# Ordering the second graph's edges between the running sums of the first layer, with those sums written out

## The chip, the cores and the metric

The kernel runs on one core of one Trainium2 chip. The metric is device time in microseconds (us) from the first to the last instruction of one execution. The core has a matrix engine (PE, whose weight loads are listed as PEld), three engines for elementwise work (DVE, ACT, POOL) and SP, which here only issues DMAs. Each runs its own instruction stream. They are ordered by semaphores alone.

## The reference, cut to what matters

```python
def gcn_layer(x, src, dst, norm, W, b, n):        # three times; 12500 nodes, 200000 edges + self loops, 256 features
    h = x @ W
    msg = h[src] * norm[:, None]
    return segment_sum(msg, dst, n) + b           # gelu after the first two
x = x + gcn3(layernorm(x), src, dst)              # the first graph
# second graph: 131072 other edges (edge_index), only the router's attention uses them
alpha = softmax over the incoming edges of leaky_relu(a_src[src2] + a_dst[dst2])
scores = layernorm(segment_sum(h[src2] * alpha, dst2) + b_gat)
x = x + sum over the top 2 of 4 experts of gate * ffn_expert(layernorm(x))
```

Both edge lists must be ordered by their target before sums over the edges of a target can be made. The order of the second graph is first used after the third layer.

## The kernel before, in words

The program is a row of blocks. At the end of a block all engines meet.

1. Constants and weights.
2. `order_second` (called in L643, body from L310): the 131072 edges of the second graph as 128 rows of 1024 keys. DVE makes one-hot tiles (L210, L212, in a loop of 64) that PE multiplies to count the edges of each target (L224). Then comes a bitonic sort: `exchange` (L231, L232) is one min and one max over 128x512, with a wait on DVE's own semaphore behind it; fourteen times PE transposes the keys (L305, 8 transposes) and DVE reads them back from PSUM (L238 to L240). Its tiles lie in `acc`, a large SBUF tile.
3. `order_first`: the same preparation for the first graph, whose edges arrive sorted, so the sort is skipped. It starts with loads of the edges, and DVE waits for them (L509).
4. Normalisation of x and the table of features in HBM.
5. `layer(l)` (L741), three times. Partition p of the core walks over 1563 edges of its own. POOL issues one indirect DMA for each edge column (L824: 128 rows of 256 floats from `feature_table`), 16 of them to a chunk, into one of four row buffers (`rows_in`). DVE makes the running sum, one instruction for each edge column (L896): state = state * keep + row, into PSUM, 16 states. After each sum DVE waits on its own semaphore `s_c`. ACT copies four states at a time to one of four output buffers (L777), `sums_out`, two in `acc` and two in `work`, and stages the next indices for POOL (L769, `put`). SP writes each chunk, 2 MB, to HBM (L961). POOL may fill a row buffer again when DVE has counted it as used (`s_used`) and ACT has staged its indices. On DVE the chunks are a hardware loop (`dve.Fori(0, LAPS)`, 24 laps of 4 chunks, 64 sums in its body), followed by three smaller chunks written out (16, 8 and 3 sums). ACT, POOL and SP loop in the same way. After the sums the layer gathers one row per node (L853) and does its matmuls (L869, L879), the node part.
6. The attention table, then one large block: POOL's 1024 gathers for the second graph (L1205) beside the experts' matmuls on PE (L1284, L1294, a loop of two node pairs per lap), and at the end the router and the weighted sum of the experts on DVE (L1501 to L1576, written out, beside 98 gathers of L1220).

## Time and profile before

| | us |
|---|---|
| median of 3 runs (11795.35 to 11846.04) | 11817.82 |
| the profiled execution, its own time | 11829.28 |
| its span in the trace | 11827.6 |
| POOL busy | 5887.5 (50%) |
| DVE busy | 3860.8 (33%) |
| PE busy | 2554.4 (22%) |
| ACT busy | 1826.5 (15%) |

The span is the time from the first to the last instruction of one profiled execution. An engine's busy time leaves out register, branch and semaphore instructions and the issuing of DMAs by queues other than POOL's indirect ones. No engine is busy for more than half of the span, so the shares name no bottleneck, and each stage has to be read by itself. In the timelines a line is an instruction (or a run of equal ones), and the bracket at its end is the idle time of its engine ahead of it, with what ended it. "issue" is idle time that ended with nothing that the profile shows.

### The profile page before, as it was taken

To read this page: it belongs to the slowest core of one execution; us is meant where nothing else is said; L and a number is where in the kernel's file an instruction comes from. 1 tells how busy PE (TensorE), PEld (TensorE's weight loads), DVE (VectorE), ACT (ScalarE), POOL (GpSimd) and SP (SyncE) were. 2 spreads that over 40 slices of the span, in tenths; PEclk is the share of its full clock that TensorE was granted. 3 is DMA by queue.
4 is the path that set the end of the run, shared out by engine and by line. 5 is a ranking of instruction groups with operands and counts; after the bars stand their busy time and mean duration, and the time that the engine had idled before them with its cause. 6 is when DMAs were issued, how large, how long until landed. Compare 5 with 4: busy or idle time off the path is not lost. (4 is left out here: it accounts for less than half of the span.)

```text
span 11827.6 us, 59944 instructions
## 1 busy us (share of the span) xinstructions
PE 2554.4 (22%) x11366; PEld 2079.0 (18%) x11366; DVE 3860.8 (33%) x7516; ACT 1826.5 (15%) x2792; POOL 5887.5 (50%) x6228
## 2 busy tenths in 40 slices
PE   6090000000040000000030000000262766655570
PEld 5070000000030000000030000000151655444460
DVE  7574333333332333333333333333340111100127
ACT  0000111111131111111131111111110111111120
POOL 0003666666636666666646666666437233344411
PEclk9999999999985555555565555555665877777785
DMA  0005555555554555555555555555441111111127
GB/s 15 9 0 162 180 180 191 179 180 186 177 168 158 182 186 180 176 183 176 180 161 174 183 183 177 182 175 191 157 140 24 36 37 37 34 34 34 34 85 223
DMA packets 586804, 1580.96 MB, mean 134 GB/s; under 512 B 134656, under 2 KB 373580, under 8 KB 547948
## 3 DMA queue, kind: packets, MB, share of 16 engines
q1 hardware_dynamic: 306828, 897.27, 21.2%
q0 software_dynamic: 278608, 668.34, 19.2%
q10 hardware_dynamic: 1296, 14.68, 0.3%
q14 instruction: 62, 0.51, 0.0%
q8 instruction: 10, 0.16, 0.0%
HBM read 820.05 MB, written 759.77 MB: 134 GB/s over the span
## 5 line engine op out<-in xcount | busy, mean ns | idle before, releaser
L824 POOL DMA_INDIRECT acc<-feature_table,staged_indices x4608 | 4356.3, 945 | 3043.4 <-issue 1523.7
L896 DVE SCALAR_TENSOR_TENSOR ps<-ps,keep_within_node,acc 128x256 f32<-128x256 f32 x4689 | 2311.4, 493 | 4521.2 <-issue 3756.1
L1205 POOL DMA_INDIRECT acc<-attention_table,idx x1024 | 972.6, 950 | 1312.5 <-DVEq L1422 978.1
L862 PE MATMUL ps<-work,carry_from_partition 128*128 128x256 f32 x6 | 3.7, 713 | 6986.2 <-ACT work L777 6986.2
L862 PEld LDWEIGHTS ps<-work,carry_from_partition 128*128 128x128 f32 x6 | 1.5, 309 | 6987.2 <-ACT work L777 6987.2
L777 ACT COPY acc<-ps 128x1024 f32<-128x1024 f32 x594 | 601.1, 1012 | 3249.0 <-remote 1664.4
L777 ACT COPY work<-ps 128x1024 f32<-128x1024 f32 x579 | 585.3, 1011 | 2370.9 <-remote 1006.0
L1284 PE MATMUL ps<-work 128*128 128x256 f32 x3136 | 801.8, 402 | 524.8 <-issue 451.1
L1294 PE MATMUL ps<-work,onehot 128*128 128x256 f32 x3136 | 783.2, 394 | 544.5 <-issue 501.1
L1384 DVE TENSOR_TENSOR acc<-ps,work 128x512 f32<-128x512 f32 x196 | 135.4, 691 | 2329.6 <-DMA feature_table<-acc 1057.0
L1284 PEld LDWEIGHTS ps<-work 128*128 128x128 f32 x3136 | 630.9, 202 | 681.2 <-issue 522.3
L1294 PEld LDWEIGHTS ps<-work,onehot 128*128 128x128 f32 x3136 | 617.1, 197 | 681.5 <-issue 562.4
L1328 ACT ACTIVATE work<-ps,eb_sb 128x256 f32<-128x256 f32 x784 | 307.0, 474 | 2212.5 <-remote 1022.0
L224 PE MATMUL ps<-onehot 128*128 128x98 bf16 x2592 | 477.4, 365 | 19.1 <-DVE onehot L212 19.1
L224 PEld LDWEIGHTS ps<-onehot 128*128 128x128 bf16 x2592 | 378.7, 146 | 117.5 <-DVE onehot L212 19.6
L879 PE MATMUL ps<-gw_sb,work 128*128 128x256 f32 x1176 | 307.1, 408 | 317.2 <-issue 214.0
L853 POOL DMA_INDIRECT acc<-unning_features_of_edges,last_edge_of_gnn_node x294 | 278.6, 948 | 94.2 <-issue 88.7
L879 PEld LDWEIGHTS ps<-gw_sb,work 128*128 128x128 f32 x1176 | 230.3, 206 | 352.5 <-issue 320.5
L932 DVE SCALAR_TENSOR_TENSOR work<-ps,dinv,gb_sb 128x256 f32<-128x256 f32 x294 | 128.5, 479 | 406.1 <-remote 345.5
L210 DVE TENSOR_TENSOR onehot<-work,acc 128x2048 bf16<-128x2048 bf16 x162 | 198.6, 1226 | 133.4 <-PE ps L224 132.5
L498 POOL IOTA acc<- 128x1563 f32 x1 | 1.4, 1442 | 470.4 <-POOLq L82 470.4
L1047 POOL DMA_INDIRECT et_scores_at_first_edges<-HG,first_edge_of_node x98 | 96.1, 980 | 235.7 <-DVE HG L1038 209.1
(308 smaller groups left out, 2226.4 us busy)
## 6 DMA issues: line engine op xcount, KB each, us to landing
unning_features_of_edges<-acc SPq DMA_DIRECT2D x147, 2048.0 KB
unning_features_of_edges<-work SPq DMA_DIRECT2D x144, 2048.0 KB
acc<-feature_table,staged_indices POOLq DMA_INDIRECT x4608
expert_rows<-acc SPq DMA_DIRECT2D x196, 256.0 KB
onehot<-feature_table SPq DMA_DIRECT2D x147, 256.0 KB
acc<-expert_rows SPq DMA_DIRECT2D x25, 1024.0 KB, 6.5
feature_table<-acc SPq DMA_DIRECT2D x98, 256.0 KB
work<-expert_rows SPq DMA_DIRECT2D x24, 1024.0 KB, 7.2
```

What stands on the lines that cost most here:

```text
L210: nc.vector.tensor_tensor(lo[a], iota_rep[0:rows], lo16[0:rows, at].unsqueeze(1).broadcast_to([rows, P, U]), ALU.is_equal)
L224: mm = nc.tensor.matmul(to, lo[a][:, :, k], hi[a][:, :, k], start=False, stop=False)
L777: nc.scalar.copy(sums_out[r][:, 4 * j:4 * j + w].rearrange("p c f -> p (c f)"), ps[:, 2 * j:2 * j + 2].rearrange("p a f -> p (a f)")[:, 0: ...
L824: nc.gpsimd.indirect_dma_start(out=rows_in[r][:, k], out_offset=None, in_=table, in_offset=bass.IndirectOffsetOnAxis(ap=staged[:, r, k:k + ...
L853: nc.gpsimd.indirect_dma_start(out=acc[:, b * D:(b + 1) * D], out_offset=None, in_=sums_dram, in_offset=bass.IndirectOffsetOnAxis(ap=take1 ...
L879: mm = nc.tensor.matmul(ps[:, 4 + r, a * D:(a + 1) * D], zt[:, r, a, k * P:(k + 1) * P], gw_sb[:, l, k], start=(k == 0), stop=(k == KD - 1 ...
L896: nc.vector.scalar_tensor_tensor(state[k], state[k - 1 if k else before], keep1[:, bass.ds(c + k, 1)], rows_in[r][:, k], ALU.mult, ALU.add ...
L1205: nc.gpsimd.indirect_dma_start(out=rows[:, i % 2, c], out_offset=None, in_=gat_table, in_offset=bass.IndirectOffsetOnAxis(ap=idx[1][:, i * ...
L1284: mm = nc.tensor.matmul(to, hid[:, x % 2, m, a * P:(a + 1) * P], w2[:, x, m], start=(m == 0), stop=(m == KH - 1), skip_group_check=True)
L1294: mm = nc.tensor.matmul(ps[:, 2 * (x % 2) + m // 2, (m % 2) * 2 * P:(m % 2 + 1) * 2 * P], w1[:, x, k, m * P:(m + 1) * P], xt[:, r, :, k], ...
L1328: ge = nc.scalar.activation(hid[:, x % 2, m], ps[:, 2 * (x % 2) + m // 2, (m % 2) * 2 * P:(m % 2 + 1) * 2 * P], ACT.Gelu, bias=b1[:, x, m: ...
L1384: nc.vector.tensor_tensor(yst[:, x], ps[:, 4 + x % 2].rearrange("p (a f) -> p a f", a=2), b2[:, x].unsqueeze(1).broadcast_to([P, 2, D]), A ...
```

## The change

The block `order_second` is gone. Its work becomes a class `SecondGraph`, and its DVE part is a Python generator: at each `yield` it hands back control. `layer(0)` takes the DVE loop over chunks apart (it is written out in all three layers now) and asks for one step of the generator after every fourth running sum. A step is one one-hot pair, one exchange, or a few small operations. PE's part (`count_hots`, `turn_keys` and four small matmuls) is put in front of PE's other work in layer 0, SP's four DMAs in front of SP's. POOL's two iotas go to `order_first`.

To make room in layer 0, the running sums there keep 8 states in PSUM banks 0 to 3 (16 before), banks 4 to 7 belong to the second graph, and the sums leave through two output buffers (four before). The tiles of the second graph lie in `work` and `HG`. In all layers ACT waits for `s_c` itself, so DVE's extra increments of `s_sum` are gone, and the index of `keep1` and the waited-for values are constants on DVE. Cut to its core:

```diff
-            with nc.Block() as block:                     # order_second: a block of its own
-                @block.vector
-                def _(dve): ...                           # hots, counts, sort, ends, prefix
-            end_phase()
+        class SecondGraph:
+            def on_sync(self, sp): ...                    # two edge loads, two DMAs of zeros
+            def on_tensor(self, pe):
+                count_hots(pe, P, COLS2 // U, ps[:, 5, 0:NB], self.s_hot, self.s_used, self.s_cnt)
+                turn_keys(pe, self.keys, COLS2, self.s_turn, self.s_back, 4)
...
+            def on_vector(self, dve):                     # a generator
...
+                for h in range(C // U):
+                    yield
+                    dve.wait_ge(self.s_used, h + 1)
+                    nc.vector.tensor_tensor(lo[h % 2], ..., ALU.is_equal)
+                    nc.vector.tensor_tensor(hi[h % 2], ..., ALU.is_equal).then_inc(self.s_hot, 1)
...
 def sort_keys(...):
                 for j in range(k - 1, -1, -1):
                     link(exchange(a, b, 1 << j))
                     a, b = b, a
+                    yield
...
                     dve.sem_inc(s_turn, 1)
                     turned += 1
+                    yield
                     dve.wait_ge(s_back, turned)
...
-        order_second()
         order_first(src, dst)
...
 def layer(l):
+            sums_out = outs[0:2] if l == 0 else outs
+            HELD = 8 if l == 0 else U
+            FREE = HELD // 4
...
-                    with dve.Fori(0, LAPS) as g:
-                        for r in range(4):
-                            sums(g * 4 + r, r, g, U, g * (4 * U) + r * U, r * U)
-                        dve.sem_clear(s_c)
+                    between = second.on_vector(dve) if l == 0 else iter(())
+                    for m, r, uses, size, c in [(m, m % 4, m // 4, U, m * U) for m in range(4 * LAPS)] + tails:
                         dve.wait_ge(s_row[r], uses * (16 * U) + (row_base[r] + 16 * size))
                         for k in range(size):
                             if k % 4 == 0:
-                                dve.wait_ge(s_free, m * 4 + (k // 4 + 1))
+                                dve.wait_ge(s_free, FREE + held_by[slot])
+                            dve.wait_ge(s_c, c + k + 1)
                             nc.vector.scalar_tensor_tensor(
-                                state[k], state[k - 1 if k else before], keep1[:, bass.ds(c + k, 1)], rows_in[r][:, k],
+                                state[k % HELD], state[(k - 1) % HELD if k else before], keep1[:, c + k:c + k + 1], rows_in[r][:, k],
                                 ALU.mult, ALU.add).then_inc(s_c, 1)
-                            dve.wait_ge(s_c, seen + k + 1)
-                            if k % 4 == 0:
-                                dve.sem_inc(s_sum, 1)
+                            if k % 4 == 3:
+                                next(between, None)
```

## Rows read from the trace of the kernel before

**Rows 1.** Windows: stretch, its length, busy time per engine (instructions), clock, DMA share, GB/s.

```profile
0.00:484.00 484.00, 219.82 (x1148) 174.52 (x1148) 376.45 (x538) 0.00 (x0) 4.00 (x16) 1.00 0.03 9
...
1053.00:3300.00 2247.00, 0.00 (x0) 0.00 (x0) 770.45 (x1563) 404.24 (x482) 1461.56 (x1546) 1.00 0.53 181
...
3576.00:5840.00 2264.00, 1.22 (x2) 0.50 (x2) 770.47 (x1563) 405.03 (x483) 1461.54 (x1546) 0.50 0.53 180
...
6113.00:8380.00 2267.00, 1.22 (x2) 0.50 (x2) 770.47 (x1563) 405.03 (x483) 1462.02 (x1547) 0.50 0.53 180
```

**Rows 2.** Groups of instructions in the sums of the first layer, 1053 to 3300.

```profile
L824 POOL DMA_INDIRECT acc<-feature_table,staged_indices x1519 | 1436.0, 945 | 738.2 <-issue 470.8 <-ACT staged_indices L769 267.3
L896 DVE SCALAR_TENSOR_TENSOR ps<-ps,keep_within_node,acc 128x256 f32<-128x256 f32 x1563 | 770.5, 493 | 1498.7 <-issue 1229.7 <-DVE ps L896 159.4 <-DMA acc<-feature_table,staged_indices 32.1
```

**Rows 3.** Timeline of POOL, the end of one run of gathers and the next.

```profile
2026.55 0.95 POOL L824 DMA_INDIRECT acc<-feature_table,staged_indices  x1 [0.30 <-issue]
2027.80 0.94 POOL L824 DMA_INDIRECT acc<-feature_table,staged_indices  x1 [0.30 <-issue]
2040.95 0.94 POOL L824 DMA_INDIRECT acc<-feature_table,staged_indices  x1 [12.21 <-ACT staged_indices L769]
```

**Rows 4.** Timeline of DVE: the first sum of five chunks in a row.

```profile
2005.34 0.49 DVE L896 SCALAR_TENSOR_TENSOR ps<-ps,keep_within_node,acc 128x256 f32<-128x256 f32 x1 [7.91 <-issue]
...
2038.33 0.49 DVE L896 SCALAR_TENSOR_TENSOR ps<-ps,keep_within_node,acc 128x256 f32<-128x256 f32 x1 [0.97 <-DVE ps L896]
...
2049.49 0.49 DVE L896 SCALAR_TENSOR_TENSOR ps<-ps,keep_within_node,acc 128x256 f32<-128x256 f32 x1 [0.36 <-issue]
...
2060.56 0.49 DVE L896 SCALAR_TENSOR_TENSOR ps<-ps,keep_within_node,acc 128x256 f32<-128x256 f32 x1 [0.36 <-issue]
...
2097.95 0.49 DVE L896 SCALAR_TENSOR_TENSOR ps<-ps,keep_within_node,acc 128x256 f32<-128x256 f32 x1 [7.92 <-issue]
```

**Rows 5.** Timeline of DVE at the last gathers of the program: written-out code.

```profile
11551.07 0.19 DVE L1546 TENSOR_TENSOR acc<-gates 128x16 f32<-128x16 f32 x1 [1.21 <-DVE acc L1549]
11552.47 0.19 DVE L1547 TENSOR_TENSOR acc<-acc 128x16 f32<-128x16 f32 x1 [1.21 <-issue]
11553.87 0.19 DVE L1548 TENSOR_TENSOR acc<-gates 128x16 f32<-128x16 f32 x1 [1.21 <-issue]
...
11636.46 0.20 DVE L1546 TENSOR_TENSOR acc<-gates 128x26 f32<-128x26 f32 x1
11636.70 0.20 DVE L1547 TENSOR_TENSOR acc<-acc 128x26 f32<-128x26 f32 x1
```

**Rows 6.** Timeline of POOL: the last gather of the program.

```profile
11603.02 0.94 POOL L1220 DMA_INDIRECT acc<-running_sums_of_edges,last_edge_of_node  x1 [0.31 <-issue]
```

**Rows 7.** Windows in the experts' block, with gathers and without.

```profile
9393.00:9556.00 163.00, 47.82 (x133) 30.62 (x132) 6.61 (x16) 6.26 (x16) 120.44 (x128) 0.57 0.12 16
9580.00:9710.00 130.00, 130.00 (x604) 114.45 (x603) 23.10 (x33) 34.73 (x80) 0.00 (x0) 1.00 0.16 54
```

**Rows 8.** Timeline of DVE: written-out sums behind the first layer's loop.

```profile
3284.80 2.08 DVE L896 SCALAR_TENSOR_TENSOR ps<-ps,keep_within_node,acc 128x256 f32<-128x256 f32 x4 [0.15 <-DVE ps L896]
3287.03 2.08 DVE L896 SCALAR_TENSOR_TENSOR ps<-ps,keep_within_node,acc 128x256 f32<-128x256 f32 x4 [0.15 <-DVE ps L896]
```

**Rows 9.** Groups of instructions in the second graph's block, 11 to 484.

```profile
L224 PE MATMUL ps<-onehot 128*128 128x98 bf16 x1024 | 188.8, 365 | 13.2 <-DVE onehot L212 13.2
...
L231 DVE TENSOR_TENSOR acc<-acc 128x512 f32<-128x512 f32 x139 | 96.2, 692 | 4.8
...
L210 DVE TENSOR_TENSOR onehot<-work,acc 128x2048 bf16<-128x2048 bf16 x64 | 78.4, 1226 | 52.7 <-PE ps L224 52.3 <-DVEq L205 0.5
L212 DVE TENSOR_TENSOR onehot<-work,acc 128x1568 bf16<-128x1568 bf16 x64 | 62.0, 969 | 0.0
...
L238 DVE COPY acc<-ps 128x512 f32<-128x512 f32 x14 | 9.7, 691 | 29.7 <-PE ps L305 29.7
```

**Rows 10.** Timeline around the start of the second and the third block.

```profile
11.30 1.27 DVE L354 CAST work<-iota 128x2048 bf16<-128x2048 f32 x1 [11.30 <-PEq L161]
...
484.25 1.36 DVE L505 MEMSET acc<- 128x1563 int32 x1 [2.24 <-PEq L82]
...
583.03 1.79 DVE L509 TENSOR_TENSOR acc<-acc 128x1563 f32<-128x1563 int32 x1 [94.15 <-DMA acc<-dst_in]
```

**Rows 11.** Timeline of PE in the experts' block during gathers.

```profile
9750.27 0.58 PE L1294 MATMUL ps<-work,onehot 128*128 128x256 f32 x1 [2.21 <-issue]
9753.07 0.58 PE L1294 MATMUL ps<-work,onehot 128*128 128x256 f32 x1 [2.22 <-issue]
```

More of the change, by code:

```diff
@@ L240, in exchange_turned, with turned_banks @@
             return nc.vector.tensor_tensor(w[:, :, 1], v[:, :, 0], high, ALU.max)
-        def turned_banks(C):
+        def turned_banks(C, first):
             n = C // 512
-            return [ps[:, n * j:n * (j + 1)].rearrange("p a f -> p (a f)") for j in range(2)]
+            return [ps[:, first + n * j:first + n * (j + 1)].rearrange("p a f -> p (a f)") for j in range(2)]
         def partition_bits(link, pi, bits_i, bits, flips):
@@ L289, in sort_keys, with sorted_in, turn_keys @@
                         a, b = b, a
-            return a
-        def turn_keys(pe, keys, C, s_turn, s_back):
+                        yield
+        def sorted_in(keys, C):
+            depth = C.bit_length() - 1
+            return keys[sum(range(1, depth + 1)) + sum(j + 1 + depth for j in range(7)) & 1]
+        def turn_keys(pe, keys, C, s_turn, s_back, first=0):
             depth = C.bit_length() - 1
@@ L297, in turn_keys @@
                 a, b = b, a
-            flat = turned_banks(C)
+            flat = turned_banks(C, first)
             turned = 0
@@ L449, in order_first @@
+        second = SecondGraph()
         def order_first(src_ap, dst_ap):
@@ L530, in run @@
                     def run():
-                        at_end = keys[sum(range(1, 12)) + sum(j + 12 for j in range(7)) & 1]
+                        at_end = sorted_in(keys, CK)
                         sp.wait_ge(s_sorted, 1)
@@ L743, in layer @@
             last = l == 2
+            if l == 0:
+                second.begin()
+            sums_out = outs[0:2] if l == 0 else outs
+            S = len(sums_out)
+            HELD = 8 if l == 0 else U
+            FREE = HELD // 4
             zst, zt, ust, xin = pairs4
             n_ = f"_l{l}"
-            s_out = [sem(f"sums_out{r}" + n_) for r in range(4)]
-            s_stg, s_tick, s_c, s_sum, s_free, s_used = (sem(c + n_) for c in (
-                "indices_staged", "pool_tick", "sum_chain", "four_summed", "four_copied", "rows_used"))
+            s_out = [sem(f"sums_out{r}" + n_) for r in range(S)]
+            s_stg, s_tick, s_c, s_free, s_used = (sem(c + n_) for c in (
+                "indices_staged", "pool_tick", "columns_summed", "four_copied", "rows_used"))
             s_carry, s_fixd = sem("carries" + n_), sem("fix_done" + n_)
@@ L837, in _ @@
                             ).then_inc(s_row[r], 16)
-                    for r in range(4):
-                        pool.wait_ge(s_out[r], 16 * (1 + LAPS + sum(t[1] == r for t in tails)))
+                    for r in range(S):
+                        pool.wait_ge(s_out[r], chunks_out[r])
                     nc.gpsimd.indirect_dma_start(
@@ L992, in _ @@
                     if last:
-                        for r in range(4):
-                            sp.wait_ge(s_out[r], 16 * (1 + LAPS + sum(t[1] == r for t in tails)))
+                        for r in range(S):
+                            sp.wait_ge(s_out[r], chunks_out[r])
                     skewed(sp, PAIRS, (0, own), *([(1, load_x)] if last else []), (9, store), period=4)
                     sp.wait_ge(s_o, 16 * PAIRS)
+                    if l == 0:
+                        sp.wait_ge(second.s_z, 32)
         for l in range(3):
```

349 lines of the change are left out of this document (192 added, 157 removed).

## The prediction

> **What bounds the kernel now.** I read the windows of the stages first. The second graph's block fills 0 to 484 us, with DVE busy for 376 us, PE for 220 and the DMA engines nearly idle. The three stretches of running sums are 2247, 2264 and 2267 us long, 57% of the program, and in them POOL is busy for 65%, DVE for 34%, DMA for 53% [rows 1]. So I looked at the groups: DVE's sums take 493 ns each, but ahead of them lie 1499 us of idle time, 1230 of it "issue" [rows 2]. Neither data nor another engine ends it.
>
> The timelines say what it is. POOL issues a gather every 1.25 us while it may, so 20.0 us per chunk of 16, and then waits about 12 us for ACT's staging, which comes behind DVE's sums [rows 3]. DVE needs very different times for equal chunks: 33.0, 11.2, 11.1 and 37.4 us in one lap, 92.6 in all [rows 4]. The waits for rows and buffers stand at the heads of chunks and groups of four, yet the gaps lie between all sums, in multiples of about 0.7 us. The two quick chunks begin near the end of POOL's idle time (2028.7 to 2041.0). My reading: while POOL issues gathers back to back, DVE gets its own instructions slowly, about 0.7 us each, and when POOL has been quiet for some 10 us it gets a stock of them that runs at 0.7 us per sum and lasts for some 35 sums (32 of them are the two quick chunks). Two other places show the same. PE issues 133 matmuls in 163 us beside 128 gathers, and 604 in 130 us without any [rows 7]. DVE's code at the program's end, written out, takes 1.40 us for an operation and the wait behind it, and 0.24 us once the last gather is gone [rows 5, 6].
>
> So the sums are bound by a balance. With n chunks per stock, slow chunks of 35.2 us (the mean of 33.0 and 37.4), and a stock that saves some 53 us (35 sums, 2.2 chunks, at 35.2 - 11.1): 35.2n - 53 = 20n + 12, n = 4.3, 22.8 us per chunk. The stage gives 2247 / 97.7 = 23.0. The model holds, and I cost the change with it.
>
> **The change part by part.**
>
> *The block removed.* `order_first` began at 484.25 and would now begin behind the constants, where the second graph's DVE work began at 11.3: 473 us less [rows 10]. What is moved to its head (a cast of 1.27 us, two POOL iotas) lies under DVE's wait of 94 us for the edges [rows 10]. SP's four DMAs go to layer 0, where DVE asks for the edges in its third step, behind eight sums that wait for the first gathers anyhow. I cost these at nothing; without that cover it would be some us once.
>
> *The sums written out, layers 1 and 2.* No trace shows this code under gathers for long, so I count instructions. A sum is the operation and a wait, 1.40 us by the rate of [rows 5], 22.4 per chunk; four waits for free states and three instructions per chunk add 7 x 0.7 = 4.9: 27.3 us in the slow pace, against 35.2 for the loop with its register arithmetic, extra increments and jump. The quick pace is 2.23 us per four sums where written out [rows 8], about 10 per chunk. If a stock is as many instructions as before (35 of 49 per 16 sums, about 110), it lasts 2.8 chunks and saves 2.8 x 17.3 = 48 us: 27.3n - 48 = 20n + 12, n = 8.2, 21.5 us. Its floor is POOL's 20.0, its ceiling 27.3, if no stock ever comes. I take 21.7, since a stock may be half passed when it arrives: 97.7 x 21.7 = 2120, about 130 to 145 us less per layer. I use 130, so 260 for two.
>
> *Layer 0.* The generator has about 254 steps (64 one-hot pairs, 153 exchanges, the rest small) for 390 groups of four, so 63.5 chunks carry four steps each and 34 carry none. The steps hold about 860 DVE instructions, 13.5 per chunk, 9.5 us in the slow pace: 36.8 us. Quick, a chunk takes 10 + 376/63.5 = 16 us [rows 1], below POOL's 20. A stock is 110 of 52 per chunk, 2.1 chunks, and saves 44: 36.8n - 44 = 20n + 12, n = 3.3, 23.6 us. So 63.5 x 23.6 + 34 x 21.7 = 2236, as the 2247 of now. On top come waits that are new inside the sums: DVE waits in line for PE, with the rest of the sums, `s_used` and so POOL's next buffer queued behind it. A one-hot pair costs PE 16 matmuls, about 3 us in the quick pace (64 pairs, 189 us [rows 9]), against 5 us or more between steps; a turn of the keys costs DVE 2.1 us of waiting now (29.7 / 14 [rows 9]) and has a group of sums ahead of its wait. Two output buffers for four: a 2 MB write must land before the chunk after next starts to leave, which has 20 us or more, and less only inside a stock. I take 80 us for these together, from 0 (all covered) to 350 (below).
>
> The Trainium skill speaks against such steps: SBUF — State Buffer, section "SBUF: two separate sides", says that DVE operations in a 2-port mode keep GpSimd from writing the descriptors of its DMAs. That would be a rival, priced below from rows.
>
> *Sum.* -473 + 80 - 260 = -653, for the profiled execution 11829.3 - 653 = 11176, and for the median, which is 11.5 lower than it, 11165 us. PE's clock in the node parts, fewer semaphores, and all later stages I leave as they are; nothing of them is changed.
>
> **The rivals.**
>
> *All code quick.* Written-out code could be fetched ahead, whatever POOL does. Then POOL's 1563 x 1.25 = 1954 us bound each layer, 293, 310 and 313 less than now, layer 0 too since its quick chunk of 16 is below 20: 473 + 916 less, about 10,430. For it: the 27 written-out sums behind the loop run at 0.56 us each [rows 8]; but they are fewer than one stock. Against it: [rows 5], written out and slow. The Trainium skill, Runtime: NRT & Kernel Launch, section "Instruction fetch mechanics", would have it so: it says that fetching is hidden in sequential code and that branches break it. By that rule the sum would be this rival's; the trace disagrees for written-out code beside gathers.
>
> *No stock comes (slower than before).* A slow chunk now leaves POOL 27.3 - 20 = 7.3 us idle, where stocks came after 10 to 12 in one piece [rows 3]. If idle time does not add up over chunks, layers 1 and 2 stay at 27.3: 2667 each, +803; layer 0's step chunks (16.8 idle) still get theirs, its other 34 cost +190. In all -473 + 80 + 803 + 190 = +600, about 12,420. It decides from 24.9 us per chunk in all three layers' plain chunks on. Against it: the balance of now, where the idle time sets itself as long as it has to be.
>
> *The written-out sums gain nothing* (the rate per instruction is worse, or a stock smaller, in straight code): -473 + 80, about 11,425.
>
> *PE is starved too.* At 2.8 us per matmul [rows 11] a pair takes 45 us and a turn 22. Blocked DVE makes POOL idle, which frees PE, so a chunk goes to perhaps 33 us for the 16 chunks of pairs (+150), and 14 turns cost up to 14 us more each (+200): about 11,165 + 350 - 80 = 11,435. For it: PE's record in [rows 7]. Against it: the pair loop is a quarter of the experts' loop in matmuls, perhaps small enough to stay within a stock.
>
> *DVE's steps hold POOL up* by their whole busy time: 376 us over 63.5 chunks, 5.9 each, the chunk 36.8n - 44 = 25.9n + 12, n = 5.1, 28.2 us, +290: 11,455. Against it: gathers stand 1.25 us apart beside DVE's sums [rows 3].
>
> **How the numbers follow.** My case 0.52 (its own range 10,950 to 11,380: step chunks of 22 to 26 us, plain ones of 20.8 to 22.7), all quick 0.08, no stock 0.07, no gain from writing out 0.13, PE starved 0.15, POOL held up 0.05. The last three lie at 11,425 to 11,455 with a spread of 100, so 10,830 to 11,560 leaves out the first two rivals and a little more. Faster by over 0.5% (59 us, about what a measurement of this kernel can tell from no change): 0.91. Within: 0.02, slower: 0.07, which is the rival without stocks.
>
> **What would show it.** `order_first` starting near 11 us; layer 1 and 2's sums in about 2120 us each, with slow gaps of 1.4 us per sum and quick runs of 45 to 50 sums; DVE's "issue" idle still there; layer 0's sums near 2320. Plain chunks at 20.0 us with POOL without pauses would be the first rival, at 27 the second; DVE waiting for L224 or L305 by some us per step, the fourth; gathers further apart than 1.25 us beside L231 and L210, the fifth. The weakest step is the stock: I have seen how it behaves in a loop only.

## The result and the profile after

The changed kernel takes 11,181.6 us (median of 4 runs, 11,174.5 to 11,191.2) against 11,827.0 us before (4 runs): ratio 0.946, 95% interval 0.943 to 0.948. I had predicted 11,165 us. Its profiled execution has a span of 11,175.9 us, 651.7 less than before. Three lines of its page, the engine totals and the two costliest groups; [rows 2] are the same two groups before, in one layer:

```profile
PE 2578.6 (23%) x11366; PEld 2084.4 (19%) x11366; DVE 3833.7 (34%) x7516; ACT 1827.4 (16%) x2792; POOL 6320.8 (57%) x6228
...
L878 POOL DMA_INDIRECT acc<-feature_table,staged_indices x4608 | 4778.3, 1037 | 2453.8 <-issue 2044.3
L955 DVE SCALAR_TENSOR_TENSOR ps<-ps,keep_within_node,acc 128x256 f32<-128x256 f32 x4689 | 2310.5, 493 | 3763.3 <-DVE ps L955 1896.6
```

A gather, 945 ns long before [rows 2], is 1037 ns long now. The windows of the stages, with the columns of [rows 1]: the head, then the sums of layers 0, 1 and 2.

```profile
0.00:484.00 484.00, 292.88 (x1583) 232.65 (x1583) 272.29 (x338) 1.66 (x2) 4.26 (x16) 1.00 0.11 35
578.00:2834.00 2256.00, 231.79 (x1146) 169.16 (x1146) 1118.16 (x2100) 404.65 (x482) 1555.71 (x1546) 1.00 0.53 180
3110.00:5275.00 2165.00, 0.00 (x0) 0.00 (x0) 770.31 (x1563) 404.37 (x482) 1609.33 (x1546) 0.50 0.55 188
5550.00:7714.00 2164.00, 0.00 (x0) 0.00 (x0) 770.23 (x1563) 404.32 (x482) 1649.59 (x1546) 0.50 0.55 188
```

The block has gone from the head, its 537 additional DVE instructions and PE's 1146 matmuls stand in layer 0. Layer 0 is 9 us longer than before (2255 us from its first sum to its last, 2246 before), layers 1 and 2 are 96 and 94 us shorter (2164.2 and 2163.4, before 2260.4 and 2257.0).

The shortening doesn't look as I had foreseen. Groups in layer 1, first of its first nine chunks, then of the rest:

```profile
L878 POOL DMA_INDIRECT acc<-feature_table,staged_indices x144 | 136.6, 949 | 43.9 <-issue 43.9
L955 DVE SCALAR_TENSOR_TENSOR ps<-ps,keep_within_node,acc 128x256 f32<-128x256 f32 x144 | 71.0, 493 | 130.2 <-DMA acc<-feature_table,staged_indices 95.2 <-DVE ps L955 18.2 <-issue 6.7
...
L878 POOL DMA_INDIRECT acc<-feature_table,staged_indices x1368 | 1437.4, 1051 | 475.5 <-issue 475.5
L955 DVE SCALAR_TENSOR_TENSOR ps<-ps,keep_within_node,acc 128x256 f32<-128x256 f32 x1412 | 695.9, 493 | 1279.5 <-DVE ps L955 796.8 <-remote 285.5 <-issue 186.7
```

For nine chunks POOL issues a gather every 1.25 us, DVE sums at 0.54 us and waits for rows, 20.0 us per chunk. Then, to the end of the layer, every chunk takes 22.4 us: DVE spends 1.40 us on a sum in the mean, and POOL's gathers have become longer (1051 ns) and stand 1.40 us apart in the mean. POOL has no pause for ACT's staging any more ([rows 3] show one of 12.21 us before), its idle time is the 0.35 us in the mean between two gathers. Nowhere in these two layers is there a run of quick sums behind a pause. The timeline of that state:

```profile
4003.10 0.94 POOL L878 DMA_INDIRECT acc<-feature_table,staged_indices  x1 [0.30 <-issue]
4003.80 0.49 DVE L955 SCALAR_TENSOR_TENSOR ps<-ps,keep_within_node,acc 128x256 f32<-128x256 f32 x1 [0.91 <-DVE ps L955]
...
4005.21 0.49 DVE L955 SCALAR_TENSOR_TENSOR ps<-ps,keep_within_node,acc 128x256 f32<-128x256 f32 x1 [0.92 <-DVE ps L955]
...
4009.54 1.24 POOL L878 DMA_INDIRECT acc<-feature_table,staged_indices  x1 [0.30 <-issue]
```

So the sum of the prediction came out, and the questions are which of its terms did, what a sum's 1.40 us are made of, and who paces the 22.4 us.

### The profile page after: what moved, and what is told of

Its sections match the earlier page's. It is cut to its first block and busy times, and to the rows that moved or that the text cites. A ratio compares the mean times of both kernels' runs of the same rounds, so it can differ in the third digit from the quotient of the medians.

```text
span 11175.9 us, 53498 instructions
## 1 busy us (share of the span) xinstructions
PE 2578.6 (23%) x11366; PEld 2084.4 (19%) x11366; DVE 3833.7 (34%) x7516; ACT 1827.4 (16%) x2792; POOL 6320.8 (57%) x6228
## 3 DMA queue, kind: packets, MB, share of 16 engines
q0 software_dynamic: 278608, 668.34, 20.8%
## 5 line engine op out<-in xcount | busy, mean ns | idle before, releaser
L878 POOL DMA_INDIRECT acc<-feature_table,staged_indices x4608 | 4778.3, 1037 | 2453.8 <-issue 2044.3
L833 ACT COPY acc<-ps 128x1024 f32<-128x1024 f32 (+1 forms) x787 | 796.7, 1012 | 3706.7 <-DVE ps L955 3204.3
L833 ACT COPY work<-ps 128x1024 f32<-128x1024 f32 (+1 forms) x386 | 390.2, 1011 | 1736.1 <-DVE ps L955 1671.5
L224 PE MATMUL ps<-onehot 128*128 128x98 bf16 x2592 | 490.4, 366 | 324.4 <-DVE onehot L406 273.4
L224 PEld LDWEIGHTS ps<-onehot 128*128 128x128 bf16 x2592 | 373.8, 147 | 440.7 <-DVE onehot L406 294.7
L312 PE MATMUL ps<-ident,work 128*128 128x128 f32 x112 | 27.6, 427 | 866.2 <-DVEq L282 641.9
```

Of the source, the lines that this page charges most:

```text
L224: mm = nc.tensor.matmul(to, lo[a][:, :, k], hi[a][:, :, k], start=False, stop=False)
L833: nc.scalar.copy(sums_out[slot][:, 4 * j:4 * j + w].rearrange("p c f -> p (c f)"), ps[:, b:b + 2].rearrange("p a f -> p (a f)")[:, 0:w * D ...
L878: nc.gpsimd.indirect_dma_start(out=rows_in[r][:, k], out_offset=None, in_=table, in_offset=bass.IndirectOffsetOnAxis(ap=staged[:, r, k:k + ...
```

## The experiments

### Each half of the change alone, and a different chip

`unroll_only` writes the sums out in all three layers, with sixteen places and four slots, and puts the second graph back as a block ahead of `order_first`:

```
+        def order_second():
+            second.begin()
+            with nc.Block() as block: ...   # on_sync, the two iotas, on_tensor, and all steps of on_vector in a row
+            end_phase()
+        order_second()
         order_first(src, dst)
...
-            sums_out = outs[0:2] if l == 0 else outs
-            HELD = 8 if l == 0 else U
+            sums_out = outs
+            HELD = U
```

> The second graph's ordering stands again as a block of its own ahead of the first graph's, and all three layers keep the written-out sums with sixteen places and four slots. The prediction gave 130 us to each written-out layer: by its terms 11,827 less three times 130 is 11,437 us. The trace of the changed kernel shows 96 and 94 us instead in layers 1 and 2, so by that reading, with the same for layer 0, this kernel takes 11,827 less 285, about 11,542 us, and its layer 0 sums take about 2,163 us, at a uniform 22.4 us per chunk of 16. By the rival that writing out gains nothing the time is about 11,827 us.

`moved_only` keeps the steps in the written-out layer 0 and gives layers 1 and 2 the loop of before:

```
                     if l == 0: ...                     # written out, with the steps
+                    else:
+                        with dve.Fori(0, LAPS) as g:
+                            for r in range(4):
+                                sums(g * 4 + r, r, g, U, g * (4 * U) + r * U, r * U)
+                            dve.sem_clear(s_c)
```

> Layers 1 and 2 go back to the hardware loop with one semaphore for every four sums; layer 0 stays as in the changed kernel, with the second graph's steps. If writing out is worth what the trace of the changed kernel shows (96 and 94 us), this takes 11,182 plus 190, about 11,372 us; by the prediction's 130 us each, 11,442 us; if the changed form gained only through something shared with layer 0, 11,182 us.

Two more went with them, on the price of an instruction. `extra_instruction`:

```
                                 ALU.mult, ALU.add).then_inc(s_c, 1)
+                            if l > 0:
+                                dve.sem_inc(s_more, 1)
```

> Behind each sum of layers 1 and 2 DVE carries one instruction more, an increment of a semaphore that nobody waits for. Theory of the instruction's price (the prediction's: an instruction costs DVE about 0.7 us or more beside the gathers): a sum then takes 2.1 to 2.8 us instead of 1.40, a chunk of 16 takes 34 to 45 us and each of the two layers 1,100 to 2,200 us longer, so the kernel takes 13,400 to 15,600 us. Rival, the price is that of a wait answered by the engine's own semaphore: the increment costs its own few tens of ns, a sum stays at 1.40 us, and the kernel at about 11,182 us.

`no_chain_wait`:

```
-                            dve.wait_ge(s_c, c + k + 1)
+                            if l == 0 or c + k == 0:
+                                dve.wait_ge(s_c, c + k + 1)
...
-    state[k % HELD], state[(k - 1) % HELD if k else before], keep1...
+    state[k % HELD], state[(k - 1) % HELD if k else before] if l == 0 else state[k % HELD], keep1...
```

> In layers 1 and 2 a sum no longer reads the sum before it but the old content of its own place, and so doesn't wait for it; it still adds the row, still increments, and is as wide. So each sum is one instruction, as before, but without a wait on DVE's own semaphore; this leaves the running sum itself out. Theory of the instruction's price: DVE stays at 1.40 us per sum, 22.4 us per chunk, and the kernel at about 11,182 us. Rival, the price of a wait: a sum goes at 0.3 to 0.6 us, DVE waits for rows, the gathers go back to 1.25 us, a chunk takes 20.1 us, each of the layers about 1,960 us, and the kernel about 10,780 us.

Measured: 9,330.8, 8,914.6, 8,914.0 and 8,926.9 us, beside 9,336.6 us for the kernel before on the same chip. This chip runs the kernel before in 21% less time, and not by its clock: in the three layers of `unroll_only` it granted what the other chip did (1.00 in the first, 0.50 in the two others). The ratios are 0.9998 (0.9989 to 1.0008) for writing out alone and 0.9553 (0.9537 to 0.9569) for moving alone. The groups in a stretch of a layer, first written out (`unroll_only`, layer 0, 1300 to 3000), then the loop (`moved_only`, layer 1, 3000 to 3400):

```profile
L903 POOL DMA_INDIRECT acc<-feature_table,staged_indices x1325 | 1253.2, 946 | 403.7 <-issue 403.7
L978 DVE SCALAR_TENSOR_TENSOR ps<-ps,keep_within_node,acc 128x256 f32<-128x256 f32 x1366 | 672.9, 493 | 1022.3 <-DMA acc<-feature_table,staged_indices 944.9 <-DMA acc<-feature_table,idx 14.0 <-DVE ps L978 1.2
```

```profile
L884 POOL DMA_INDIRECT acc<-feature_table,staged_indices x321 | 303.5, 946 | 97.8 <-issue 97.8
L982 DVE SCALAR_TENSOR_TENSOR ps<-ps,keep_within_node,acc 128x256 f32<-128x256 f32 x320 | 157.7, 493 | 242.3 <-DMA acc<-feature_table,staged_indices 185.4 <-DVE ps L982 33.7
```

The operations and the gathers are as long as in [rows 2]; what is missing is the "issue" time ahead of DVE's sums. POOL paces every chunk at 20.0 us, DVE waits for rows in either form, so writing out gains nothing, and an instruction more or a wait less leaves the time within 13 us of `moved_only`'s. The theories that these two runs were to part, the price of an instruction and the price of a wait, were not tested here. This is my first rival, "all code quick", but as a trait of the chip and not of written-out code.

### The changed kernel again, and half the slots

`changed_again` is the changed kernel itself. `half_slots` gives layers 1 and 2 eight places and two slots too (`sums_out = outs[0:2]`, `HELD = 8`).

> The changed kernel as it is, beside the kernel before on the same chip. The four kernels run so far took 8,914 to 9,331 us on a chip where the kernel before took 9,337 us, not 11,827 us; there the sums of every layer went at the pace of the gathers, 20.0 us per chunk of 16, in the loop and written out. Reading one, the slow supply of instructions beside gathers is a property of the chip that a program lands on: where the kernel before takes about 11,830 us this one takes about 11,180 us (ratio 0.945), and where it takes about 9,337 us this one takes about 8,914 us (ratio 0.955, the block of the second graph alone). Reading two, the written-out sums gain or lose something of their own there too: a ratio outside 0.953 to 0.957 beside 9,337 us.

> Layers 1 and 2 too keep eight running sums and two slots for the copies. The prediction gave the halved slots no price of their own, since a copy of four sums takes 1.0 us out of the 5 to 5.6 us in which the next four are made: the same time as the changed kernel within 0.3% on either kind of chip. Rival, ACT's copies or the transfers of two slots bind: layers 1 and 2 longer by more than 1 us per chunk, 200 us in all.

They ran on another chip: before 11,840.4 us, the changed kernel 11,211.2 (ratio 0.947, 0.945 to 0.949), half the slots 11,198.1 us in one run. So there are two kinds of chip. The later runs met the slower kind three more times (before at 11,793, 11,812 and 11,821 us, on three further chips) and the quicker kind once more (9,338 us, on a second chip of it). The rows of the prediction are from the slower kind, and it has to be judged there. Halving the places and slots costs nothing: layers 1 and 2 are 2166.0 and 2167.5 us long there, 2165.4 and 2166.5 with all of them.

### The price of a sum

Three kernels meant for the slower kind ran on a quick chip. `wait_or_count` has the edit of `no_chain_wait` in layer 1 and that of `extra_instruction` in layer 2. `other_gathers` changes who brings the rows, `plain_loop_narrow` is `unroll_only` with the old loop in layer 1 and a narrow sum in layer 2:

```
+    if l == 1:                               # other_gathers: ACT in place of POOL
+        act.wait_ge(s_used, m + 1)
+        for k in range(size):
+            nc.scalar.dma_start(rows_in[r][:, k], table[k * P:(k + 1) * P]).then_inc(s_plain[r], 16)
-    for k in range(U):
+    for k in range(0, U, 2 if l == 2 else 1):
         nc.gpsimd.indirect_dma_start(...)
...
+    w = slice(0, 64 if l == 2 else D)        # plain_loop_narrow
+    nc.vector.scalar_tensor_tensor(state[k % HELD][:, w], ..., rows_in[r][:, k, w], ...)
```

> Two of the edits so far, one in each layer, for a chip of the slower kind (kernel before at about 11,830 us). Layer 1: a sum reads the old content of its own place and doesn't wait for the sum before it, which leaves the running sum itself out; one instruction per sum, no wait on DVE's own semaphore. Layer 2: behind each sum one increment more that nobody waits for. Layer 0 is that of the changed kernel (2,255 us). If the price is per instruction, layer 1 stays at 22.4 us per chunk (2,164 us) and layer 2 goes to 34 to 45 us per chunk (3,300 to 4,300 us). If the price is that of the wait, layer 1 goes to 20.1 us per chunk (1,960 us) with the gathers 1.25 us apart, and layer 2 stays at 22.4. On a chip of the quicker kind both stay at 20.0 us.

> Layer 1: its rows come by plain transfers of 128 rows of 1 KB each, issued by ACT, as many and as large as the gathers, while POOL does nothing; the rows are not those of the edges, so the layer's values are left out. Layer 2: POOL gathers only every second row of a chunk (8 instead of 16), DVE makes all 16 sums. If POOL's gathers slow the supply of DVE's instructions, layer 1's sums run at 0.54 us, 8.6 us per chunk, or at the pace of ACT's copies and issues, well under 20 us per chunk. If the transfers themselves slow it, layer 1's sums stay at 1.40 us, 22.4 us per chunk. Layer 2: if DVE's 1.40 us per sum is what binds a chunk, it stays at 22.4 us; if the gathers bind it and DVE only follows, it falls towards 10 us; a value between means that DVE is quick while POOL pauses, as the prediction has it. On a chip of the quicker kind both fall: layer 2 to about 10 us.

> The second graph's ordering is a block of its own again. Layer 0: written-out sums, sixteen places, no steps of the second graph between them. Layer 1: the hardware loop of the kernel before. Layer 2: written out, but a sum covers 64 of its 256 elements, which leaves three quarters of the sums out; the instructions are as many. Expected on a chip of the slower kind: layer 0 about 2,163 us (22.4 us per chunk), so that the steps of the second graph cost the difference to 2,255 us, about 92 us (the prediction: 80 of stepping over a base of 2,236); layer 1 about 2,258 us. Layer 2: if the width of DVE's operations is what stretches the gathers from 1.25 to 1.40 us, they go back to 1.25 us and POOL pauses or the chunk takes about 20 us; if the supply of instructions paces both, it stays at 22.4 us with the gathers at 1.40.

They took 8,917.2, 7,366.0 and 9,336.1 us beside 9,337.8 for the kernel before: 20.0 us per chunk in all forms with 16 gathers, 13.9 us with plain transfers, 10.1 us with half the gathers. I then put the same edits into stretches of one kernel, so that one run is enough:

```
+    KINDS = ("as_is", "no_wait", "old_wait", "extra", "narrow")
+    kind_of = lambda m: KINDS[min(4, m // 20)] if l == 1 else "as_is"
+    own = kind in ("no_wait", "old_wait")
+    if kind == "old_wait":
+        dve.wait_ge(s_c, c + k + 1 - 4)
+    elif kind != "no_wait":
+        dve.wait_ge(s_c, c + k + 1)
...                                    # the sum: from state[k] if own, 64 wide if narrow
+    if kind == "extra":
+        dve.sem_inc(s_more, 1)
...                                    # POOL, layer 2: laps 2 to 8 every second row; 9 to 15 none, ACT:
+    nc.scalar.dma_start(rows_in[r][:, k], table[k * P:(k + 1) * P]).then_inc(s_plain[r], 16)
```

> The changed kernel, with the written-out sums of layers 1 and 2 changed by stretches of chunks, so that one run shows several edits beside each other; the running sums of the changed stretches are left out. Layer 1: chunks 0 to 19 as they are; 20 to 39 a sum reads the old content of its own place and carries no wait; 40 to 59 the same with a wait for the sum four before, met long since; 60 to 79 as they are with one more increment behind each sum, which nobody waits for; 80 to 98 a sum covers 64 of 256 elements. Layer 2: laps 0 and 1 as they are, laps 2 to 8 with every second row gathered, laps 9 to 15 with plain transfers from ACT in place of POOL's gathers, laps 16 to 23 as they are. On a chip of the slower kind the stretches as they are take 22.4 us per chunk. Theory of the instruction's price: 22.4 without a wait and with an old one, 34 to 45 with the extra increment, 22.4 narrow. Rival, price of the wait: 20.0 us without one, 22.4 with the extra increment; the old wait tells whether it is having a wait or waiting that costs. Rival, width: 20.0 narrow. Layer 2: if the gathers slow the supply, the half gathers give between 10 and 22 us, and the plain transfers well under 20 us; if the transfers slow it, 22.4 us. On a chip of the quicker kind all stay at 20.0 us except the halved (10 to 11 us) and the plain ones (about 9 to 15 us).

It ran on the slower kind. From the starts of the sums in the trace, as medians over the chunks of a stretch: how long DVE takes from the first sum of a chunk to its sixteenth, how far the first sum is behind the one before it, and the mean length of a chunk.

| stretch | first sum to sixteenth | ahead of the first sum | chunk |
|---|---|---|---|
| as it is (chunks 10 to 19) | 20.8 us | 1.6 | 22.4 us |
| no wait (20 to 39) | 12.4 | 10.0, for rows | 22.4 |
| old wait (40 to 59) | 15.9 | 6.5, for rows | 22.4 |
| one increment more (63 to 71) | 25.9 | 3.5 | 29.4 |
| 64 elements wide (83 to 90) | 20.8 | 1.6 | 22.4 |
| half the gathers (layer 2, 12 to 33) | 9.6 (8.1 to 17.8) | 0.7 | 11.4 |
| plain transfers (layer 2, 40 to 61) | 8.1 | 6.0, for ACT's copies | 13.9 |

The timeline of DVE in this kernel: two sums as it is, the first chunk without the wait, the end of a later one and the start of the next, and three sums with the increment:

```profile
3536.49 0.49 DVE L978 SCALAR_TENSOR_TENSOR ps<-ps,keep_within_node,acc 128x256 f32<-128x256 f32 x1 [0.91 <-issue]
3537.89 0.49 DVE L978 SCALAR_TENSOR_TENSOR ps<-ps,keep_within_node,acc 128x256 f32<-128x256 f32 x1 [0.91 <-issue]
3539.47 3.78 DVE L978 SCALAR_TENSOR_TENSOR ps<-ps,keep_within_node,acc 128x256 f32<-128x256 f32 x9 [1.08 <-DVE ps L978]
3544.86 0.49 DVE L978 SCALAR_TENSOR_TENSOR ps<-ps,keep_within_node,acc 128x256 f32<-128x256 f32 x1 [1.61 <-issue]
...
3751.36 0.49 DVE L978 SCALAR_TENSOR_TENSOR ps<-ps,keep_within_node,acc 128x256 f32<-128x256 f32 x1 [0.91 <-issue]
3752.76 0.49 DVE L978 SCALAR_TENSOR_TENSOR ps<-ps,keep_within_node,acc 128x256 f32<-128x256 f32 x1 [0.91 <-issue]
3753.47 0.49 DVE L978 SCALAR_TENSOR_TENSOR ps<-ps,keep_within_node,acc 128x256 f32<-128x256 f32 x1 [0.22 <-issue]
3763.47 3.77 DVE L978 SCALAR_TENSOR_TENSOR ps<-ps,keep_within_node,acc 128x256 f32<-128x256 f32 x9 [9.51 <-remote]
...
4658.63 0.49 DVE L978 SCALAR_TENSOR_TENSOR ps<-ps,keep_within_node,acc 128x256 f32<-128x256 f32 x1 [1.61 <-issue]
4660.03 0.49 DVE L978 SCALAR_TENSOR_TENSOR ps<-ps,keep_within_node,acc 128x256 f32<-128x256 f32 x1 [0.90 <-DVE ps L978]
4662.12 0.49 DVE L978 SCALAR_TENSOR_TENSOR ps<-ps,keep_within_node,acc 128x256 f32<-128x256 f32 x1 [1.60 <-issue]
```

Four things follow. DVE's work isn't the price: a quarter of the width changes nothing. An instruction more costs: the increments put 7.0 us on a chunk, 0.44 us each, less than the 0.7 us of the prediction; a chunk took 29.4 us, where I had expected 34 or more. The wait costs too: without it the sixteen sums take 12.4 us, with one that was met long since 15.9, with the one on the sum just before 20.8, so 0.2 us per sum for having a wait and 0.3 more for waiting freshly. So the rival "price of a wait" is true in part. The chunks of 22.4 us without a wait, which I had expected from the price of the instruction alone, come from POOL's gathers, which bind there. And it isn't a stock that DVE gathers while it stands still: the first chunk without the wait, with a gap of 1.08 us ahead of it, starts with the same nine sums at 0.41 us as the later ones behind 9.5 us (3539.47 and 3763.47), and takes 13.1 us, where they take 12.4.

Single distances come in steps of about 0.7 us (0.7, 1.4 and 2.1) in every slow stretch, also without a wait, where 1.40 is the most frequent one. That does not make 0.70 us the price of an instruction. In the trace a sum carries its wait in its own record, so the written-out chunk has 21 DVE instructions where the prediction counted 39, the one with increments 37, and a chunk of the loop before 42: 22.4 us over 21 is 1.07 us, 29.4 over 37 is 0.79. What makes the steps, no run shows.

That the gathers cause the slow pace, and not the bytes they bring, is shown by the stretch in which POOL rests and as many rows of the same size come by plain transfers. Groups of this kernel, 6050 to 6430:

```profile
L978 DVE SCALAR_TENSOR_TENSOR ps<-ps,keep_within_node,acc 128x256 f32<-128x256 f32 x432 | 212.9, 493 | 167.1 <-ACT work L839 74.5 <-ACT acc L839 72.8
```

Most of DVE's idle time ends with ACT's copies, next to none of it is "issue", and the chunk takes 13.9 us on either kind of chip.

### Who paces the 22.4 us

Without its waits DVE makes its sums in 12.4 us per chunk and then waits for rows, and yet a chunk takes 22.4 us: there POOL is what binds. `mixed_two` tests what binds POOL, and also spreads the steps in layer 0:

```
+    few = l == 2 and 20 <= m < 60            # DVE: one sum in four, then_inc(s_c, 4)
+    if few and k % 4:
+        continue
...
-    if k % 4 == 3:
+    if k % 4 == 3 and (4 * m + k // 4) * 256 % 388 < 256:
         next(between, None)
...
+    if more:                                 # POOL, layer 1, laps 5 to 14, behind each gather
+        pool.sem_inc(s_more, 1)
```

> The changed kernel with three edits, for a chip of the slower kind. Theory, from the run before this: beside gathers an instruction costs the engine that draws it about 0.70 us, a gather on POOL is two such (1.40 us, 22.4 us per chunk) as soon as POOL has run long without a pause, so in layers 1 and 2 of the changed kernel POOL itself is the bound and DVE follows it closely. Layer 1: in laps 5 to 14 POOL carries one increment more behind each gather, which nobody waits for. The theory gives three instructions per gather, 2.1 us, 33.6 us per chunk; rival, the gathers are stretched by something in their transfers or by DVE's writes and an increment costs some tens of ns: about 22.4 to 24 us. Layer 2: in chunks 20 to 59 DVE makes one sum in four (the other sums are left out). The theory gives 22.4 us per chunk, as POOL has the same work; if DVE's sums bind or stretch the gathers, the chunk falls to 20.0 us. Layer 0: the steps of the second graph are spread evenly over all 388 groups of sums instead of the first 250: by the mean of the chunks with steps (24.2 us) and without (21.2 us) about 23.2 us per chunk, 2,266 us in all against 2,255 us, so within 30 us of it; if the runs of quick sums depend on how closely the steps follow each other, it is off by more. On a chip of the quicker kind layers 0 and 2 and the unchanged laps go at 20.0 us per chunk, the changed laps at 20.0 to 22 us.

Groups of layer 2, 5900 to 6300, with one sum in four:

```profile
L879 POOL DMA_INDIRECT acc<-feature_table,staged_indices x286 | 297.3, 1040 | 103.1 <-issue 103.1
L962 DVE SCALAR_TENSOR_TENSOR ps<-ps,keep_within_node,acc 128x256 f32<-128x256 f32 x108 | 53.2, 492 | 343.8 <-DMA acc<-feature_table,staged_indices 294.2 <-DVE ps L962 28.1 <-issue 8.9
```

286 gathers in 400 us are 1.40 us each, 22.4 us per chunk, while DVE waits for rows for 294 of 400 us. So in the steady state it isn't DVE that stretches the gathers: POOL is slow by itself there. My theory for that, a gather as two instructions of 0.70 us, fell in the same run: with one more instruction per gather a chunk took 22.7 us in the mean of 40, not 33.6, in a mixture of chunks at 20.0 us and of others up to 28 us with stops between gathers like these (POOL's timeline, layer 1):

```profile
3892.96 0.94 POOL L879 DMA_INDIRECT acc<-feature_table,staged_indices  x1 [4.33 <-issue]
...
3897.72 0.95 POOL L879 DMA_INDIRECT acc<-feature_table,staged_indices  x1 [3.81 <-issue]
```

What a pause does for POOL shows in `mixed`, where it stood still for 4 to 10 us at a time while DVE worked through the chunks with increments (stops at 4683 to 4817 us). Behind them its gathers were back at 1.25 us and a chunk of 16 took it 20.0 to 20.3 us, ten times in a row, and only then 22.4 us again. A layer's start gives it ten such chunks. So POOL has something that a rest refills; what it is, and why it costs just 2.4 us per chunk, stays open; a backlog in the transfers that a rest works off would look the same and was not tested. DVE shows the same 22.4 us on its own in the stretch of narrow sums: in chunks 83 to 87 POOL was quick and up to four buffers ahead, and DVE took 22.4 us for each. Why the two engines' paces are equal is not shown.

Spreading the steps made layer 0 2238 us long, against 2255 to 2274 us in the four traces that have it as the changed kernel has: 17 to 36 us less, in one run, where I had expected 11 us more. The whole of `mixed_two` took 11,155.6 us, the kernel before beside it 11,811.8.

### Writing out alone, on the slower kind

> The kernel with the second graph's block back in its place and all three layers written out, once more, for a chip of the slower kind. From the traces of the changed kernel and of the two runs with stretches: 22.4 us per chunk in layers 1 and 2 from the ninth chunk on, 2,163 us each; if layer 0 without steps goes the same way it takes 2,163 us as well, the steps of the second graph cost 92 us there, and the kernel takes 11,827 less 280 to 290, about 11,540 us (ratio 0.975 to 0.977). If layer 0 without steps is as long as with them (2,255 us), the steps cost nothing and the kernel takes about 11,635 us. On a chip of the quicker kind the ratio is 1.000, as measured.

11,561.1 us, ratio 0.978 (0.976 to 0.980) to 11,820.9. Windows of its head and its three layers:

```profile
0.00:484.00 484.00, 219.83 (x1148) 174.51 (x1148) 374.88 (x532) 0.00 (x0) 3.87 (x15) 1.00 0.03 9
1057.00:3222.00 2165.00, 0.00 (x0) 0.00 (x0) 770.38 (x1563) 404.43 (x482) 1608.49 (x1546) 1.00 0.54 188
3496.00:5661.00 2165.00, 0.00 (x0) 0.00 (x0) 770.40 (x1563) 404.33 (x482) 1649.52 (x1546) 0.50 0.55 188
5933.00:8099.00 2166.00, 0.00 (x0) 0.00 (x0) 770.32 (x1563) 404.31 (x482) 1609.42 (x1546) 0.50 0.54 188
```

Layer 0 without steps takes 2164.0 us like the others, though its PE clock is at the upper level and theirs at the lower, so the clock has no part in it. The steps cost 2255 - 2164 = 91 us, and up to 110 by the other traces of the changed layer 0. Writing out is worth 82, 97 and 93 us against the loop, 272 by the traces and 260 by the clock of whole runs.

On the quick chip the steps cost 57 us (`moved_only`'s layer 0 is 1993.8 us long, 1937.3 without steps in `unroll_only`), 27 of them in the first 18 chunks, which hold the one-hot pairs, and 30 in the chunks with the sort. Groups of `moved_only`, 578 to 945:

```profile
L884 POOL DMA_INDIRECT acc<-feature_table,staged_indices x273 | 283.9, 1040 | 83.2 <-issue 83.2
...
L404 DVE TENSOR_TENSOR onehot<-work,HG 128x2048 bf16<-128x2048 bf16 x62 | 75.4, 1215 | 0.0
...
L406 DVE TENSOR_TENSOR onehot<-work,HG 128x1568 bf16<-128x1568 bf16 x62 | 60.1, 969 | 0.0
```

Beside the one-hot operations a gather takes 1040 ns, 987 ns beside the sort's, 946 ns in the layers without steps. A chunk takes 21.6, 20.7 and 20.0 us.

On the slower kind nearly all of the cost comes with the one-hot pairs, and it is DVE waiting for PE. Groups of the changed kernel, 578 to 2100, and DVE's timeline there:

```profile
L404 DVE TENSOR_TENSOR onehot<-work,HG 128x2048 bf16<-128x2048 bf16 x64 | 78.0, 1219 | 185.7 <-remote 173.3 <-PE ps L224 12.4
...
L238 DVE COPY work<-ps 128x512 f32<-128x512 f32 x14 | 9.5, 681 | 0.0
```

```profile
645.38 2.07 DVE L955 SCALAR_TENSOR_TENSOR ps<-ps,keep_within_node,acc 128x256 f32<-128x256 f32 x4
686.06 1.22 DVE L404 TENSOR_TENSOR onehot<-work,HG 128x2048 bf16<-128x2048 bf16 x1 [38.60 <-remote]
```

The profile names PE for only 12.4 of the 185.7 us and calls the rest "remote". But the instruction (L404) waits for one semaphore only, which besides a first increment of DVE's own nothing raises but the last matmul of a pair (L224), and in the trace each of the 25 waits ends within 0.1 us of a rise of it. So DVE waited for PE, up to 38.6 us at a time. The rise comes 3 to 50 us behind the end that the profile gives for the matmul that it stands for; what holds it up is not shown. The other three traces with this layer 0 on the slower kind have 176 to 196 us of such idle time, the five on quick chips none. Chunk 18, the first behind the pairs, starts 130 to 132 us later than in `unroll_again`, counted from the layer's first sum, in all four traces. The sort's 46 chunks add at most 5 us to that, and the chunks without steps behind it give 18 to 38 us back.

## Why the prediction was right, and where it was not

**The block: right.** 473 us less, measured 472.4 (`order_first`'s first instruction starts at 11.84 us, before at 484.25 [rows 10]). What moved to its head cost nothing.

**Layer 0: 71 us too long, from two wrong parts.** I had 2236 us for written-out sums with steps, and 80 for waits that the steps bring, +80 in all; measured +9. By the prediction's own terms written-out sums alone would be 97.7 x 21.7 = 2120 us and the steps 116 + 80 = 196. Measured are 2164 and 91, so the base was 44 us too short and the steps about twice too dear. Within the steps the parts came out otherwise, too. The 80 was for DVE waiting in line for PE, and that wait was there and larger: 186 us ahead of the one-hot pairs, none ahead of the turned keys. What wasn't there is the 116, the steps' own instructions in the slow pace: the sort's 46 chunks are hardly longer than plain ones.

The chunks with steps take 24.1 to 24.3 us in the mean (predicted 23.6 plus the waits), mostly in turns of 13 to 16 and 30 to 38 us. The slow pace and the quick chunks around POOL's pauses are there as the prediction had them, since DVE's work and waits are longer than 22.4 us and POOL does pause.

**Layers 1 and 2: the direction right, the mechanism wrong.** Predicted 130 us less each, measured 96 and 94. The pace of a sum held, 1.40 us in the mean, but not its explanation. "A sum is the operation and a wait, 1.40 us by the rate of [rows 5]" makes it two instructions of 0.7 us; the trace has one instruction for both, an increment more cost 0.44 us, and taking the wait away saved 0.5 us per sum, most of it only if the wait was a fresh one. Two steps behind it failed. First, "four waits for free states and three instructions per chunk add 7 x 0.7 = 4.9: 27.3 us in the slow pace": where DVE had rows enough and was alone the bound (`mixed`, chunks 83 to 87), a chunk took 22.4 us, so these seven cost nothing beside the sums. Second, and this is what I had not seen, "20n + 12": I took POOL's 1.25 us per gather as given whenever it may issue. The 1.25 us hold for the first ten chunks or so behind a rest. As the written-out DVE no longer falls behind, POOL no longer rests, and it then takes 22.4 us per chunk by itself. With no pause of POOL there are no quick chunks for DVE either. The layer is two paces of 22.4 us, where I had an alternation with a mean of 21.7; that is 2164 instead of 2120 us.

**The sum.** Predicted -473 + 80 - 260 = -653, measured -472.4 + 9 - 190 = -653, and +2 in the rest. The 71 us too much in layer 0 and the 70 us too much gain in layers 1 and 2 cancel, so the 11,165 us owes its closeness in part to luck. The range would have held it with either error alone.

**The rivals.** All quick: false where the prediction was made, true on the two quick chips. No stock (+803): its premise came true, there are no quick chunks in layers 1 and 2, but its time did not, as the slow pace was 22.4 and not 27.3 us. No gain from writing out: false here (0.978), true on the quick chip. PE starved: true in part, and I had it at 0.15. Its sign, DVE waiting for L224 by some us per step, is there with 2.9 us per pair, and the chunks with pairs cost 130 us where this rival had 150. The 200 for the turns didn't come, and that PE lacks instructions rather than something else is not shown. DVE's steps hold POOL up: by 1.6 us per chunk on the quick chip in the stretch of the one-hot pairs, 57 us in all, not by their whole busy time; on the slower kind it can't be told from the rest of the 91 us.

The Trainium skill, SBUF — State Buffer, section "SBUF: two separate sides", says that DVE operations in a 2-port mode keep GpSimd from writing the descriptors of its DMAs. The quick chip's 1040 against 946 ns agree with it in direction only: in which mode the one-hot operations ran no run shows. The same skill, Runtime: NRT & Kernel Launch, section "Instruction fetch mechanics", says that fetching is hidden in sequential code. On the quick chip the traces agree, 0.54 us per written-out sum beside gathers; on the slower kind they don't, with 1.40 us, if it is fetching that the "issue" time stands for, which the profile doesn't say.

## What to carry to other kernels

When an engine's idle time is "issue", don't take the step of its gaps for the price of an instruction: the gaps here came in steps of 0.7 us, while an increment more cost 0.44 us, a wait more up to 0.5, and three quarters less width nothing. When the profile calls a wait "remote", look up which semaphore it is and who raises it: 173 us of waiting for PE stood under that word. Before costing a change with the pace of another engine, ask how long the trace ever shows that engine without a rest; POOL's 1.25 us per gather was true for laps with a 12 us pause and not for a whole layer. And a gain that rests on such a pace belongs to the chip it was measured on: moving the block is worth about 380 us (472 less 91) on the one kind and 422 on the other (`moved_only` against before), the written-out sums 260 us on the one and nothing on the other.

## What the runs showed of the hardware

- Two kinds of chip. The kernel before takes 9,337 and 9,338 us on two chips, and 11,793 to 11,840 us on four others. Granted clock, operations (493 ns per sum) and gathers (946 ns, 1.25 us apart) are the same; on the four, DVE's instructions come slowly while POOL issues gathers; PE's did in the kernel before [rows 11], and DVE stood 176 to 196 us waiting for PE's one-hot pairs, on the quick chips not at all. It isn't the layers alone: behind layer 2's last sum come 3,462 us in the changed kernel there, 2,102 us in `moved_only` on the quick chip. Why the chips differ no run tells.
- Beside gathers on the slower kind DVE takes 1.40 us per sum with its wait in the mean, against 0.54 us otherwise, in distances of 0.7, 1.4 and 2.1 us. Sixteen sums take 20.8 us with a fresh wait each, 15.9 with an old one, 12.4 without; an increment behind each adds 0.44 us; 10 us of DVE's own rest ahead of them make 0.7 us of difference.
- POOL's own gathers go on the slower kind from 20.0 to 22.4 us per 16 after some ten chunks without a rest, and do so even when DVE makes one sum in four.
- On both kinds a chunk fed by 16 plain transfers of 128 rows takes 13.9 us, bound by ACT, which issues them and copies.
